# Packed attention projection with two-part weights, a moved block of relative logits, and one group's selection rows written on the chip

## What is computed

```python
# layer 0, for each of 8 images (1024 tokens of 256 channels)
x = x + concat(conv3x3(gn(x), 192 outputs) + conv_b,
               attn(gn(x)) @ attn_w + attn_b)          # attn_w is 64 x 64
# attn: 8 heads of 8 channels; logits = q k + rel_w + rel_h, softmax, times v
# layer 1
t = tokens(x)
t = t + (softmax(Q K / sqrt(128)) V) @ W_o + b_o + ln(t)  # Q, K, V from ln(t); 128 units
t = t + layer_norm(mixture of 2 of 8 experts of ln(t) + ln(t))
```

## Time and profile before

| what | us |
|---|---|
| median of 3 runs | 2121.3 (2120.63 to 2123.63) |
| the profiled execution, its own time | 2120.94 |
| span of its trace, first to last instruction | 2118.9 |
| PE matmul busy in the span | 2019.7 (95%) |
| DVE busy | 1406.9 (66%) |
| ACT busy | 1283.4 (61%) |
| POOL busy | 255.5 (12%) |
| mean granted TensorE clock, share of full | 0.977 |

### The profile page before, as it was taken

One profiled execution on the slowest core, in us unless ns is written; L12 is line 12 of the kernel. 1 busy time (PEld: TensorE's weight loads), 2 busy tenths in 40 slices (PEclk: granted clock), 3 DMA queues, 4 the chain that ended last, 5 costly groups with the idle time before them and its releaser, 6 DMA issues. The chain is left out here.

```text
span 2118.9 us, 27713 instructions
## 1 busy us (share of the span) xinstructions
PE 2019.7 (95%) x10112; PEld 1389.4 (66%) x10112; DVE 1406.9 (66%) x2075; ACT 1283.4 (61%) x2205; POOL 255.5 (12%) x277
## 2 busy tenths in 40 slices
PE   5999999987999999999999999999999969999997
PEld 4788887753445455444455446888888848888886
DVE  6776675675777777777777745666666545556655
ACT  4344444355777677777777766766666635556654
POOL 2000000002222222222222400000000000001000
PEclk9999998998999999999999999999999979999999
DMA  3334548797677777776666522333331154433341
GB/s 114 100 90 159 189 155 199 201 262 97 100 114 113 107 111 114 107 128 108 113 113 106 168 91 79 109 110 115 115 109 56 51 188 185 154 145 140 143 155 50
DMA packets 144070, 268.08 MB, mean 127 GB/s; under 512 B 23488, under 2 KB 87744, under 8 KB 139968
## 3 DMA queue, kind: packets, MB, share of 16 engines
q1 hardware_dynamic: 136128, 241.12, 47.6%
q0 software_dynamic: 7680, 25.17, 3.8%
q10 hardware_dynamic: 128, 0.03, 0.0%
HBM read 156.37 MB, written 107.24 MB: 124 GB/s over the span
## 5 line engine op out<-in xcount | busy, mean ns | idle before, releaser
L850 DVE TENSOR_REDUCE a_nmax<-a_sm 128x1 f32<-128x1024 f32 x512 | 603.4, 1219 | 193.5 <-PE a_sm L870 193.1
L1139 ACT ACTIVATE p_shared<-a_st 128x512 f32<-128x512 f32 x1024 | 556.9, 597 | 253.2 <-PE a_st L1167 252.0
L1182 PE MATMUL a_pv<-p_shared,a_va 128*32 128x512 f32 x2048 | 273.0, 606 | 0.0
L1167 PE MATMUL a_st<-a_qf,a_kf 121*128 121x512 f32 x704 | 252.1, 438 | 4.4 <-PEq L1206 3.3
L1167 PEld LDWEIGHTS a_st<-a_qf,a_kf 121*128 121x128 f32 x704 | 119.0, 189 | 197.7 <-ACT p_shared L1139 185.9
L870 PE MATMUL a_sm<-a_kf,a_qf 120*128 120x512 f32 x704 | 199.9, 401 | 1.9 <-PEq L250 1.8
L2182 DVE SCALAR_TENSOR_TENSOR x_h_lo<-x_hid,x_wts,x_h_hi 128x512 fp32r<-128x512 f32 x128 | 95.8, 750 | 140.0 <-ACT x_h_hi L2143 139.9
L2272 PE MATMUL x_h_ps<-x_v_hi,x_w 128*128 128x512 f32 x512 | 183.3, 399 | 0.0
L2286 PE MATMUL x_y_ps<-x_h_hi,x_w 128*128 128x512 f32 x512 | 180.8, 394 | 0.0
L2139 ACT ACTIVATE x_hid<-x_h_ps,x_bias 128x512 f32<-128x512 f32 x128 | 88.4, 691 | 139.7 <-PE x_h_ps L2272 139.7
L870 PEld LDWEIGHTS a_sm<-a_kf,a_qf 120*128 120x128 f32 x704 | 129.5, 190 | 38.3 <-issue 7.1
(11 more groups left out here) (302 smaller groups left out, 3414.6 us busy)
## 6 DMA issues: line engine op xcount, KB each, us to landing
x_w<-w_d SPq DMA_DIRECT2D x31, 1024.0 KB, 9.1
rel_d<-p_shared SPq DMA_DIRECT2D x12, 2048.0 KB, 11.5
a_qf<-rel_d SPq DMA_DIRECT2D x22, 512.0 KB
a_qf<-rel_d SPq DMA_DIRECT2D x44, 256.0 KB
c_xtok<-in_x SPq DMA_DIRECT2D x8, 1024.0 KB, 6.7
va_d<-c_va SPq DMA_DIRECT2D x16, 512.0 KB, 6.5
a_va<-va_d SPq DMA_DIRECT2D x32, 256.0 KB, 24.6
a_w_st<-in_L_ffn_W POOLq DMA_DIRECT2D x32, 256.0 KB, 7.6
```

What stands on the lines that cost most here:

```text
L850: nc.vector.tensor_reduce(nmax[:, h, t:t + 1], sm[k % 2][:], axis=AX.X, op=ALU.max, negate=True).then_inc(sm_read, 1)
L1139: nc.scalar.activation(probs[:, t % 2, h, half * HALF:(half + 1) * HALF], st[half][:], ACT.Exp).then_inc(exp_done, 1)
L1167: nc.tensor.matmul(st[half][:], kf[j][0:ROW_M + 1, h, t * P:(t + 1) * P], qf[j][0:ROW_M + 1, h, 2 * t // TT, half * HALF:(half + 1) * HALF ...
L1182: m = nc.tensor.matmul(pv[32 * h:32 * h + 32, cols], va[j][:, t, h, :], probs[:, t % 2, h, cols], start=t == 0, stop=t == TT - 1, skip_gro ...
```

## The change

It has three parts. (1) In the last image's list of units, c0 of column factor 1 stands ahead of rel 4. (2) In the first attention block SP stores r = 1 first, right after the keys of group 1, and r = 0 second; POOL waits for the landing of r = 1 and writes the selection rows of `a_kf2` by four copies; the wait and the 2 MB DMA at the head of the second block go. (3) The projection: only the 8 value rows of each head are loaded, 64 rows for half an image, and multiplied on DVE, for the first image too; DVE makes a high part and a low part, which lie above each other in the 128 rows of `b_att_hl`; the weights are made in two parts, each twice above and twice beside itself; and PE runs two f32r matmuls with 128 rows of output, the lower 64 of which are used. Eight small loads of the weights become two, and POOL's clearing goes. The order in BETWEEN stays.

```diff
-            UNITS[:4] + rel(4, 0, 8) + UNITS[4:] + rel(5, 0, 8)]
+            UNITS[:5] + rel(4, 0, 8) + UNITS[5:] + rel(5, 0, 8)]
...
                 load_keys(sp, kq_d, 1, kf[1], loaded[1])
+                store_relative(1)
                 store_relative(0)
                 load_v(sp, 1, 1)
-                store_relative(1)
                 sp.wait_ge(rel_stored[0], 32)
...
                 double_queries(pool, 1, 1)
+                pool.wait_ge(rel_stored[1], 32)
+                for h in range(HG):
+                    last = nc.gpsimd.tensor_copy(kf[BUFS - 1][:, h].rearrange("p (a n) -> p a n", a=2), group.both_halves)
+                last.then_inc(built[BUFS - 1], 1)
...
-                sp.wait_ge(rel_stored[1], 32)
-                sp.dma_start(bits(kf[BUFS - 1][:]).rearrange("p h (a n) -> p (h a) n", a=2),
-                             group.ones_hot[:].rearrange("p (a n) -> p a n", a=1).to_broadcast([P, 2 * HG, HALF])).then_inc(built[BUFS - 1], 16)
...
     def load_weighted(self, sp, n, j):
-        sp.dma_start(self.att[j][:], self.att_d[n].rearrange("g p n -> p g n")[:, :, half(j)]).then_inc(self.att_loaded[j], 16)
-        for g in range(GROUPS):
-            src = self.rsum_d[n, g].rearrange("h (a n) -> h a n", a=1)[:, :, half(j)]
-            sp.dma_start(self.rsb[j][:, g], src.to_broadcast([HG, 32, HALF])).then_inc(self.att_loaded[j], 16)
+        rows = self.att_d[n].rearrange("g (h r) n -> (g h) r n", r=32)[:, 0:DH, half(j)]
+        sp.dma_start(self.att[j][:], rows).then_inc(self.att_loaded[j], 16)
+        sums = self.rsum_d[n].rearrange("g h (a n) -> (g h) a n", a=1)[:, :, half(j)]
+        sp.dma_start(self.rsb[j][:], sums.to_broadcast([NH, DH, HALF])).then_inc(self.att_loaded[j], 16)
...
-            self.nc.gpsimd.tensor_tensor(self.att[k][:], self.att[k][:], self.rsb[k][:], ALU.mult).then_inc(self.norm_ready, 1)
...
+    def normalize(self, dve, n, k):
+
+        dve.wait_ge(self.att_loaded[k], 32 * n + 32)
+        self.nc.vector.tensor_tensor(self.att[k][:], self.att[k][:], self.rsb[k][:], ALU.mult)
+        dve.drain()
+        high = self.att_hl[k][0:DK]
+        self.nc.vector.tensor_copy(high, self.att[k][:])
+        dve.drain()
+        self.nc.vector.tensor_tensor(self.att_hl[k][DK:P], self.att[k][:], bits(high), ALU.subtract).then_inc(self.norm_ready, 1)
...
+        split_projection()
+        for k in range(2):
+            self.normalize(dve, 0, k)
         split_weights()
         project(0)
...
-                            nc.vector.tensor_tensor(att[k][:], att[k][:], rsb[k][:], ALU.mult).then_inc(norm_ready, 1)
+                            first.normalize(dve, n, k)
...
-                            for g in range(GROUPS):
-                                m = nc.tensor.matmul(b_ps[DK:P, :], wp[:, g, :], att[k][:, g, :], start=g == 0, stop=g == GROUPS - 1)
+                            for part, w in enumerate((first.wp_hi, first.wp_lo)):
+                                m = nc.tensor.matmul(b_ps[:], w[:].rearrange("p a c -> p (a c)"), first.att_hl[k][:], start=part == 0, stop=part == 1)
```

More of the change, by code:

```diff
@@ L1275, in __init__ @@
         self.x_v = x.rearrange("b h w c -> b (h w) c").rearrange("b (t p) c -> b p t c", p=P)
-        self.att = [place(f"b_att{j}", [P, GROUPS, HALF], slab + 4 * KB * j) for j in range(2)]
-        self.rsb = [place(f"b_rsb{j}", [P, GROUPS, HALF], slab + 8 * KB + 4 * KB * j) for j in range(2)]
+        self.att, self.rsb = ([place(f"b_{n}{j}", [DK, HALF], slab + at * KB + 2 * KB * j) for j in range(2)]
+                              for n, at in (("att", 0), ("rsb", 4)))
+        self.att_hl = [place(f"b_att_hl{j}", [P, HALF], slab + 8 * KB + 2 * KB * j, f32r) for j in range(2)]
         self.mixT = place("b_mixT", [P, KC, TOK], slab + 16 * KB)
@@ L1285, in __init__ @@
         self.wo, self.bo = place("b_wo", [P, C], slab + 45 * KB), place("b_bo", [P, C], slab + 46 * KB)
-        self.wp = place("b_wp", [P, GROUPS, DK], slab + 47 * KB)
+        self.wp_st = place("b_wp_st", [P, DK], slab + 12 * KB)
+        self.wp_hi, self.wp_lo = (place(f"b_wp_{n}", [P, 2, DK], slab + at * KB, f32r) for n, at in (("hi", 13), ("lo", 14)))
         self.k_lo0 = place("b_k_lo0", [P, TOK], slab + 48 * KB, f32r)
@@ L1351, in load @@
             self.load_x(sp, 0, j)
-        sp.wait_ge(self.consts, 3)
-        for g in range(GROUPS):
-            for h in range(HG):
-                sp.dma_start(self.wp[32 * h:32 * h + DH, g], self.attn_w[(g * HG + h) * DH:(g * HG + h + 1) * DH]).then_inc(self.proj_loaded, 16)
+        for i in range(2):
+            sp.dma_start(self.wp_st[DK * i:DK * (i + 1)], self.attn_w).then_inc(self.proj_loaded, 16)
         sp.dma_start(self.pb[DK:P], self.attn_b.rearrange("(p a) -> p a", a=1)).then_inc(self.proj_loaded, 16)
@@ L1374, in constants @@
         make_identity(self.nc, pool, self.ident[:], self.consts)
-    def clear_projection(self, pool):
-        self.nc.gpsimd.memset(self.wp[:], 0.0).then_inc(self.consts, 1)
     def pool(self, pool):
-        for k in range(2):
-            pool.wait_ge(self.att_loaded[k], 16 * (1 + GROUPS))
-            self.nc.gpsimd.tensor_tensor(self.att[k][:], self.att[k][:], self.rsb[k][:], ALU.mult).then_inc(self.norm_ready, 1)
         for k in range(2):
@@ L1404, in split_weights, with split_projection @@
             nc.vector.tensor_tensor(self.w_lo[:], self.w_st[:], bits(self.w_hi[:]), ALU.subtract).then_inc(self.w_split, 1)
+        def split_projection():
+            dve.wait_ge(self.proj_loaded, 16 * 3)
+            both = self.wp_st[:].rearrange("p (a c) -> p a c", a=1).to_broadcast([P, 2, DK])
+            nc.vector.tensor_copy(self.wp_hi[:], both)
+            dve.drain()
+            nc.vector.tensor_tensor(self.wp_lo[:], both, bits(self.wp_hi[:]), ALU.subtract)
         def project(k):
@@ L1487, in tensor, with project @@
         nc = self.nc
-        def project(k, g):
-            if k == g == 0:
+        def project(k, part):
+            if k == part == 0:
                 pe.sem_inc(self.a_read, 1)
                 pe.sem_inc(self.b_read, 1)
-                pe.wait_ge(self.proj_loaded, 16 * (NH + 1))
-            if g == 0:
+            if part == 0:
                 pe.wait_ge(self.norm_ready, k + 1)
                 pe.wait_ge(self.b_read, b_at("proj", k) + 1)
-            m = nc.tensor.matmul(b_ps[DK:P, :], self.wp[:, g, :], self.att[k][:, g, :], start=g == 0, stop=g == GROUPS - 1)
-            if g == GROUPS - 1:
+            m = nc.tensor.matmul(b_ps, (self.wp_hi, self.wp_lo)[part][:].rearrange("p a c -> p (a c)"), self.att_hl[k][:], start=part == 0, stop=part == 1)
+            if part == 1:
                 m.then_inc(self.b_done, 1)
@@ L1575, in self_attention @@
         free = lambda name, shape, at, dt=f32: nc.alloc_sbuf_tensor_at(name, shape, dt, offset=free_at + at * 1024)
-        ident, pb, power, wo, bo, wp = first.ident, first.pb, first.power, first.wo, first.bo, first.wp
-        w_hi, w_lo, att, rsb, mixT, xb = first.w_hi, first.w_lo, first.att, first.rsb, first.mixT, first.xb
+        ident, pb, power, wo, bo = first.ident, first.pb, first.power, first.wo, first.bo
+        w_hi, w_lo, mixT, xb = first.w_hi, first.w_lo, first.mixT, first.xb
         st6, mv, var, rstd, grow, shift = first.st6, first.mv, first.var, first.rstd, first.grow, first.shift
@@ L1595, in self_attention @@
         a_ps, b_ps, c_ps = ps("b_a_ps", 2 * C), ps("b_b_ps", HALF), ps("b_c_ps", 2 * C)
-        sums_stored, att_loaded, x_loaded = first.sums_stored, first.att_loaded, first.x_loaded
+        sums_stored, x_loaded = first.sums_stored, first.x_loaded
         mix_loaded, norm_ready, a_done, a_read, b_done, b_read = (
```

7 lines of the change are left out of this document (1 added, 6 removed).

## The result

The changed kernel takes **2100.2 us** (median of 4 runs, 2098.0 to 2106.5) against 2122.2 for the kernel before beside it; the ratio is 0.9905, 95% interval 0.9884 to 0.9926. That is faster by 20 us, inside the range, but 8 us above the forecast of 2092. Run again in a later comparison the same kernel gave 2099.2 and a ratio of 0.9899 (0.9884 to 0.9914).

A forecast was written before the change was run, and what follows sets the result against it. PE was taken as the bound in the inner attention groups and layer 1, with stalls elsewhere. Terms -10, +5.5, -12.5, -1, -1.6 and -9.2 sum to -28.8 against 2120.9, forecasting 2092 us, range 2077 to 2107.

The forecast's parts named there:

- the two rivals at 2101: Group 2's loads still come late, or DVE's added work eats layer 1's gain: 2101 each; chance 0.22, both 0.04.
- Part 1: End of the convolutions: c0 ahead of rel 4 starts the first attention block 10 us earlier, ends -13 and -7.
- Closed up, and with the last stores behind, it ends near 384: Convolutions' end: 18.6 us of DMA work from 363, without holes, plus last stores of 2.5, ends near 384.
- the change does not do what it says: Rival: the clock at 340 falls although PE is busy, losing 9 of 13 us: 2097; within the forecast's 0.55.
- Part 2a: First attention block: storing r = 1 first, with r = 0 queued behind it, lengthens the block by 5.5 us.
- my own bound of +8: First attention block: worst end of the store-order term, where POOL's four copies of 1 us come last.
- which ends at 60.7, with the landing 61.5: First attention block: stores and group 1's loads, summed from 395.5, end 60.7 us after the start, landing 61.5.
- Part 2b and clock: Second attention block: the whole 12.51 us stall before group 2 goes, -12.5, and some low clock with it, -1.
- part 3a: Last attention group: four f32 projection matmuls become cheaper f32r ones, worth -1.6 us, between 0 and -2.8.
- Part 3b: Layer 1: cheaper projections give 1.4 us in each of six inner images and 0.8 in image 0, together -9.2.
- PE's whole gain: Rival: DVE has unseen slack in step 2, so layer 1 gives 19.6 us: 2082; chance 0.13.
- Slower by the clock in layer 1: Rival: new PE pauses in step 3 of six images drop the clock to 1.2 GHz, giving 2152; chance 0.04.

The follow-up runs named there:

- experiment 1: Changed kernel with the unit order undone, c0 of column factor 1 behind rel 4 again: 2108.2 us, ratio 0.9944.
- experiment 5: Changed kernel with rel 4's store issued between the two halves of group 0's query loads, in the last image of the convolutions: 2094.5 us.
- experiment 6: Changed kernel, mix 3 moved to step 4, vvar 1 to step 3: 2101.8 us; also with old store order, rel 4's store between group 0's loads: 2083.3.
- experiment 9: Changed kernel with old store order, POOL's copies in the second block, rel 4's store between group 0's loads, and x's second half in quarters: 2080.3 us.
- experiment 3: Kernel before with only the projection change (two f32r matmuls, its loads and normalization): 2113.4 us, ratio 0.9970.
- experiment 4: Changed kernel with mix 3 of the next image moved from step 3 to the head of step 4 in layer 1: 2100.5 us.
- experiment 7: Changed kernel with the second half of the next image's x loaded as two quarters in layer 1, the first after out 2: 2093.8 us.
- experiment 2: Changed kernel with r = 0 stored first as before and POOL's wait and copies moved to the second block: 2097.1 us, ratio 0.9884.

## Why the prediction was right and wrong

The sum said -28.8; the trace gave -20.6, of which 2.0 are chance that brought it nearer. The measured 2100 lies closer to the two rivals at 2101 than to the forecast, but neither happened: no stall is left before group 2, and layer 1 gave its 9.4. By its own steps:

- **Part 1, forecast -10, measured -4.5** (experiment 1: 4.7). Near 340 the clock did what was said, and PE's share held (14.5 us earlier behind rel 4 and c0, 2.0 of them chance, for 13.1). The step that failed is "Closed up, and with the last stores behind, it ends near 384" (which is 11.5 before 395.5; the -10 is the middle of the stated ends). It treated the queue as something that bounds only the end of the block. It left out the wait inside: rel 5's first copy needs the landing of rel 4's store. Issued 7.2 us earlier behind the same loads, that store landed 1.5 us earlier, all of it chance. With part 1 undone (experiment 1) it lands at the same time. The rival "the change does not do what it says" had the low clock at the wrong place for the wrong reason. Experiment 5 took the wait away and got 5.5 us earlier.
- **Part 2a, forecast +5.5, measured +10.0.** The mechanism is right, the size was off, and beyond my own bound of +8. The step is "which ends at 60.7, with the landing 61.5", a sum of separate DMA works. The rows had the total as a measurement: r = 1 landed where SP's wait of 11.5 ended, at the issue of 463.4, which is 67.9 after 395.5. Before and after, the queue carries the same stores and loads; it took 66.1 after, and 67.8 with the order turned back in experiments 6 and 9. Whoever waits for the last of them waits for all of it. A sum of shares (27.6 and 10.6 and 20.6) misses the parts in which the DMA engines are not all busy. These parts are not the same in the two orders (before, the share is down to 0.53 from 432 to 435; after, at the end), so that the totals lie within 2 us is a finding, not something to count on.
- **Part 2b and clock, forecast -12.5 and -1; part 3a, -1.6; together -15.1, measured -14.6.** The stall went whole. Experiment 3 puts part 3a at 0.3, in one pair of traces; that the exchange of score tiles covers the rest is argued, not shown. By difference 1.8 is left for the clock in the place of 1. The time at the low clock in this stage fell from 9.7 us to 7.0, which is worth about 1.4 (an estimate, half of the difference), so two small errors met.
- **Part 3b, forecast -9.2, measured -9.4, for a reason only half right.** The pauses of PE in step 3 are there, with x landing 4.2 after its issue. But I had named two causes, DVE's unbroken row and the load. Experiments 4 and 6 followed the first and gained nothing; experiment 7 took away the second alone, and the period fell to 51.98, so 2.6 of the 2.8 us of an image were there. The rival "PE's whole gain" was a question of one load.
- **Slower by the clock in layer 1.** What I held against this rival was right: between the second image and the seventh the clock, when it fell, did so for 3.4 us. The profiled execution of the change shows no such fall, the repeated one shows one (at 1394.3, its image 2 us longer), and experiments 1, 2 and 5 one each; the traces of experiments 3, 4 and 6 show none there, and neither do the three with x in quarters, which lack the pauses. These are too few traces to say what the pauses do to the clock.
- By the Trainium skill, "DMA: Bandwidth & Descriptors", section "Queues, rings and completion order", the descriptors of a queue are consumed in ring order on each DMA engine. The trace agrees in both places: r = 1 lands at 437.9 and 445.3 and r = 0, issued behind it, at 447.9 and 455.1; rel 4's store lands 28.8 after its issue behind the loads of group 0 and 15.3 after it between them (experiment 5). Both failures were in not following the rule to the wait that stands on it.

## What to carry to other kernels

When an issue is made earlier on a queue that is already full, ask when it lands, not when it is issued, and who waits for that landing. Put behind everything only a transfer that nobody waits for soon. When a pause has two possible causes, take away one at a time: a pause that moves to the next wait when the order is edited may have a root ahead of both, here a load of which the needed half could start two steps (12.5 us) earlier.

## What the runs showed of the hardware

- The end of this queue was slower than its middle. At the end of the first block of the changed kernel, while only the last store and the last values are left, half the DMA time is idle (share 0.51, 206 GB/s, against 0.97 and 392 in the 6 us before):

```profile
441.00:447.00 6.00, 2.85 (x11) 1.47 (x9) 4.28 (x4) 0.00 (x0) 1.66 (x2) 0.92 0.97 392
447.00:456.00 9.00, 0.00 (x0) 0.00 (x0) 0.00 (x0) 0.17 (x1) 2.68 (x6) 0.50 0.51 206
```

Nine microseconds at that rate carry 1.9 MB, which the stretch before would have carried in 4.7. That is nearly the difference between my 61.5 and the 66.1. The 16 landing signals of the last store come as eight from 449.1 to 450.2 and eight from 454.0 to 455.1; why was not tried. In the kernel before, the two groups of the last store begin 1.1 us apart (461.2 and 462.3), here 4.9.
- The same pauses do not always have the same clock behind them. In experiment 2 the clock fell at 415 behind two pauses of PE of 0.7 and 0.8 us that the traces of before, of the change and of experiment 4 have as well, at full clock. It cost some 6 us. Whether this makes that kernel's spread of 16 us is not shown, since only one of its executions was traced.
